# An expert layer with arms chosen at run time: the next expert's first steps queued in front of the jumps, and waits at the first exponential moved

## The reference

```python
x = x + relu(batchnorm(aggregate(ln(x)) @ W_l.T + b_l + ln(x) @ W_r.T))   # graph stage
xf = ln(x); logits = xf @ gate_w.T + gate_b                                # route
topk_val, topk_idx = top_k(logits, 2); probs = softmax(topk_val)
for kk in range(2):
    for e in range(4):
        mask = idx == e
        eo = _expert(xf, mask, ...)        # 8 heads, keys masked by mask
        out = out + where(mask, eo * w, 0)
x = x + out

def _expert(xf, mask, ...):
    h = ln(xf) * ln1_w + ln1_b
    q, k, v = split(h @ ipw.T + ipb)
    a = softmax(where(mask, q @ k.T / sqrt(64), NEG))
    x1 = xf + (a @ v) @ opw.T + opb
    return x1 + gelu(ln2(x1) @ w1.T + b1) @ w2.T + b2
```

## Time and profile before

| | |
|---|---|
| median of 3 runs | 1213.86 us (1209.42 to 1222.64) |
| profiled execution | 1213.72 us |
| its span | 1212.0 us |
| PE busy | 986.6 us, 81% |
| DVE busy | 720.9 us, 59% |
| ACT busy | 511.5 us, 42% |
| POOL busy | 496.6 us, 41% |
| mean granted TensorE clock | 0.910 |

### The profile page before, as it was taken

The page is one execution under the profiler, slowest core; times in us unless marked ns, Lnnn a source line. Parts: engine busy times, 40 slices in busy tenths (PEclk is TensorE's granted clock), DMA queues, the critical chain, the costliest instruction groups (busy, mean ns, idle before and its releaser), DMA issues.

```text
span 1212.0 us, 25215 instructions
## 1 busy us (share of the span) xinstructions
PE 986.6 (81%) x7268; PEld 572.8 (47%) x7269; DVE 720.9 (59%) x1723; ACT 511.5 (42%) x980; POOL 496.6 (41%) x455
## 2 busy tenths in 40 slices
PE   3897899999926677877788788888888889988786
PEld 2555567788513234433444334444444445534443
DVE  4597536441483576746865665665747458646743
ACT  2301122221423356325644426685858742336631
POOL 2102434452647444204531116473838752306641
PEclk9998889998957886999878898999999899989997
DMA  5491000000357410511134110000000032200011
GB/s 162 121 272 43 2 1 0 0 0 1 136 157 197 133 54 19 210 64 35 35 124 165 59 37 19 1 2 1 0 0 0 18 136 105 92 28 2 1 35 36
DMA packets 34850, 75.88 MB, mean 63 GB/s; under 512 B 8203, under 2 KB 8501, under 8 KB 34474
## 3 DMA queue, kind: packets, MB, share of 16 engines
q1 hardware_dynamic: 26122, 55.91, 14.8%
q0 software_dynamic: 8320, 16.49, 4.4%
q10 hardware_dynamic: 288, 2.10, 0.5%
HBM read 49.06 MB, written 26.70 MB: 63 GB/s over the span
## 4 chain that ended last, share of the span: by engine, by line
PE 54%; issue 14%; DVE 11%; ACT 8%; POOL 7%; DMA 2%; DVEq 1%; SPq 1%; ACTq 1%; POOLq 0%
PE bank L1465 17%; PE bank L1306 8%; PE bank L1346 6%; POOL p_lo L778 4%; PE bank L1642 3%; DVE mx L2338 2%; PE bank L1340 2%; ACT p_all L1058 2%; PE bank L1268 2%; PE bank L1525 2%; PE bank L1566 2%; POOL lists L730 1%; DVE mx L2478 1%; PE bank L1656 1%; PE bank L1548 1%
## 5 line engine op out<-in xcount | busy, mean ns | idle before, releaser
L778 POOL TENSOR_TENSOR p_lo<-p_all,p_hi 128x512 f16<-128x512 f32 (+2 forms) x240 | 253.3, 1069 | 263.7 <-ACT p_all L1058 262.1
L1055 ACT ACTIVATE p_hi<-bank 128x512 f16<-128x512 f32 (+2 forms) x240 | 131.7, 549 | 77.0 <-PE bank L1550 29.1
L2033 DVE TENSOR_SCALAR oh_src<-iota,edge 125x1250 f16 x178 | 106.0, 595 | 89.0 <-PE bank L1306 85.6
L1058 ACT ACTIVATE p_all<-bank 128x512 f32<-128x512 f32 (+2 forms) x240 | 131.2, 547 | 3.9 <-POOL p_lo L778 2.9
L1306 PE MATMUL bank<-oh_src,oh_dst 125*125 x534 | 108.8, 356 | 3.1 <-DVE oh_dst L2035 1.5
L2338 DVE TENSOR_REDUCE mx<-bank 128x1 f32<-128x512 f32 x144 | 87.2, 655 | 27.4 <-PE bank L1525 27.0
L1642 PE MATMUL bank<-hT,w 128*128 128x512 f16 x288 | 77.7, 405 | 24.3 <-ACT t L1102 18.9
L1465 PE MATMUL bank<-hT,w 128*128 128x256 f16 (+1 forms) x552 | 93.7, 335 | 3.9 <-issue 1.9
L1306 PEld LDWEIGHTS bank<-oh_src,oh_dst 125*125 x534 | 69.8, 141 | 41.9 <-issue 20.7
L1566 PE MATMUL bank<-v_hi,p_lo 128*128 128x65 f16 (+1 forms) x832 | 67.9, 199 | 22.6 <-POOL p_lo L778 20.1
L1566 PEld LDWEIGHTS bank<-v_hi,p_hi 128*128 128x128 f16 x832 | 49.8, 101 | 68.1 <-ACT p_hi L1055 31.4
(11 more groups left out here) (335 smaller groups left out, 1964.4 us busy)
## 6 DMA issues: line engine op xcount, KB each, us to landing
w_stage<-in_ew_dram SPq DMA_DIRECT2D x40, 512.0 KB, 4.4
lists<-zeros SPq DMA_DIRECT2D x1, 10340.0 KB
x_in<-lists SPq DMA_DIRECT2D x15, 517.0 KB, 6.6
x_mem<-lists SPq DMA_DIRECT2D x3, 1024.0 KB, 5.4
x_mem<-lists SPq DMA_DIRECT2D x1, 2560.0 KB, 9.7
out_dram<-x_mem SPq DMA_DIRECT2D x10, 250.0 KB
table<-rows SPq DMA_DIRECT2D x5, 449.8 KB
big<-in_x_dram SPq DMA_DIRECT2D x10, 224.0 KB
```

The source lines that it names most:

```text
L778: nc.gpsimd.tensor_tensor(p_lo[:, b % NPB, 0:cn], p_all[:, b % NP32, 0:cn], p_hi[:, b % NPB, 0:cn], ALU.subtract).then_inc(s_lo, 1)
L1055: nc.scalar.activation(p_hi[:, b % NPB, 0:cn], stb[b % 2][:, 0:cn], ACT.Exp).then_inc(s_exp, 1)
L1058: nc.scalar.activation(p_all[:, b % NP32, 0:cn], stb[b % 2][:, 0:cn], ACT.Exp).then_inc(s_all, 1)
L2033: nc.vector.tensor_scalar(oh_src[:, bass.ds(slot, 1), i, 0:N].rearrange("p a n -> p (a n)"), iota[:, :], edge[:, 0, i, bass.ds(g, 1)], Non ...
```

## The change

Five edits. `chosen` gets a function `ahead` that is emitted in front of each choice of an arm. ScalarE queues there the rows and the affine of the first two pairs, TensorE their turns and `value(0)`, VectorE the copy of `ep` and the four splits; what they queue is taken out of the arms. In the long arm the rows of pairs 2 and 3 are now both made ahead of the affine of pair 2, and in every arm stands a dummy activation `unread_e` with Exp. `WARM_NEXT` is gone. `bias_raw` moves to the last four tiles of `o_rows`, and ScalarE waits for `s_given` where it waited for `s_bias`. In the short arms the wait for `s_scat` goes to where `oT` is first written (j == 1); GpSimd's is dropped there, and in the long arm GpSimd waits for `s_bias` ahead of its low weights. In the first short head `side_of(1, 0)` and `side_of(1, 1)` are cut in halves of six matmuls, the first of them ahead of the heads.

```diff
--- before.py
+++ after.py
@@ -58,7 +58,7 @@
 LOW = 32
-WARM_SHORT, WARM_LONG, WARM_ROUTE, WARM_TURN, WARM_NEXT = 7, 12, 31, 5, 14
+WARM_SHORT, WARM_LONG, WARM_ROUTE, WARM_TURN = 7, 12, 31, 5
 UP = 5
...
@@ -135,6 +135,8 @@
 
+    if ahead is not None:
+        ahead(engine.snap(counter, min_val=0, max_val=NE - 1))
     choose("first")
@@ -201,7 +205,7 @@
         spot = sb("spot", [TT, 1], F32)
-        raised, unread = spot[0:1, :], spot[32:64, :]
+        raised, unread, unread_e = spot[0:1, :], spot[32:64, :], spot[64:96, :]
         slots = sb("slots", [TT, NT, 2], I32)
@@ -347,13 +351,13 @@
         p_all = sb("p_all", [P, NP32, 512], F32, attention)
-        bias_raw = p_all[:, 0, :]
         groups = ExitStack()
...
         o_rows = sb("o_rows", [P, NTL, P], F32, attention)
+        bias_raw = o_rows[:, NTL - 4:NTL, :].rearrange("p t n -> p (t n)")
         halves = sb("halves", [P, 2, 2, LW], F16, attention)
@@ -791,7 +795,6 @@
                 if shape.short:
-                    pool.wait_ge(s_scat, 16 * 2 * NT)
                     for u in range(H):
@@ -799,6 +802,8 @@
                 else:
+                    pool.wait_ge(s_bias, e + 1)
+                    pool.sem_inc(s_idle, 1)
                     for p in range(QKV_P, NWP):
@@ -988,36 +993,41 @@
 
+            def first_rows(e, p):
+                act.wait_ge(s_nr[p], 16 * (e + 1))
+                for t in (2 * p, 2 * p + 1):
+                    nc.scalar.activation(normal[:, t % 4, :], x_in[:, t, 0:D], ACT.Identity,
+                                         scale=x_in[:, t, D + 1:D + 2]).then_inc(s_n1, 1)
+
+            def ahead_act(e):
+                nc.scalar.activation(unread[:, :], ident[32:64, 0:1], ACT.Identity, scale=1.0)
+                act.wait_ge(s_msplit, msplit.at(0))
+                act.wait_ge(s_ln1, e + 1)
+                for p in range(AHEAD // 2):
+                    act.wait_ge(s_ahead[p], 32)
+                    first_rows(e, p)
+                for p in range(AHEAD // 2):
+                    scaled_columns(p, ep_ln1[:, 0:KC], ep_ln1[:, KC:2 * KC])
+
             def expert_act(e, shape):
...
                 ns, nq = len(spans), len(shape.queries)
-
-                def first_rows(p):
-                    if p < AHEAD // 2:
-                        act.wait_ge(s_ahead[p], 32)
-                    if p == AHEAD // 2:
-                        act.sem_inc(s_idle, 1)
-                        with nc.scalar.If(e < 1):
-                            act.wait_ge(s_ahead[2], 16 * (nt - AHEAD))
-                    act.wait_ge(s_nr[p], 16 * (e + 1))
-                    for t in (2 * p, 2 * p + 1):
-                        nc.scalar.activation(normal[:, t % 4, :], x_in[:, t, 0:D], ACT.Identity,
-                                             scale=x_in[:, t, D + 1:D + 2]).then_inc(s_n1, 1)
 
...
 
-                nc.scalar.activation(unread[:, :], ident[32:64, 0:1], ACT.Identity, scale=1.0)
-                act.wait_ge(s_msplit, msplit.at(0))
-                act.wait_ge(s_ln1, e + 1)
-                first_rows(0)
-                first_rows(1)
-                for p in range(np):
+                if np > AHEAD // 2:
+                    with nc.scalar.If(e < 1):
+                        act.wait_ge(s_ahead[2], 16 * (nt - AHEAD))
+                    first_rows(e, 2)
+                    first_rows(e, 3)
+                nc.scalar.activation(unread_e[:, :], ident[64:96, 0:1], ACT.Exp, scale=1.0)
+                for p in range(2, np):
                     scaled_columns(p, ep_ln1[:, 0:KC], ep_ln1[:, KC:2 * KC])
                     if p + 2 < np:
-                        first_rows(p + 2)
+                        first_rows(e, p + 2)
                 turned.skip(nt)
@@ -1127,6 +1137,8 @@
                         row_of(u + 1)
+                        if j == 1:
+                            act.wait_ge(s_scat, 16 * 2 * NT)
                         if j > 0:
@@ -1157,8 +1169,7 @@
                     row_of(0)
-                    act.wait_ge(s_bias, e + 1)
-                    act.wait_ge(s_scat, 16 * 2 * NT)
+                    act.wait_ge(s_given, e + 1)
                     for u in range(H):
@@ -1474,23 +1485,29 @@
 
+            def turn_first(p):
+                pe.wait_ge(s_n1, normed1.at(2 * p + 2))
+                for q in range(2):
+                    if p > 0:
+                        pe.wait_ge(s_affine, affine.at(2 * p + q - 1))
+                    turn(p, q)
+
+            def value(t):
+                pe.wait_ge(s_hsplit, hsplit.at(2 * (t // 2) + 2))
+                if t >= 2:
+                    pe.wait_ge(s_vcopy, vcopied.at(t - 1))
+                product(stb[t % 2][:, :], lambda a, c: hT[a][:, c, t * P:(t + 1) * P],
+                        lambda b, c: w16[:, b, c * 3 * D + 2 * D:(c + 1) * 3 * D], KC).then_inc(s_v, 1)
+
+            def ahead_pe(e):
+                for p in range(AHEAD // 2):
+                    turn_first(p)
+                pe.wait_ge(s_elo, e * NWP + QKV_P)
+                value(0)
+
             def expert_pe(e, shape):
...
                 ns, nq = len(spans), len(shape.queries)
-
-                def turn_first(p):
-                    pe.wait_ge(s_n1, normed1.at(2 * p + 2))
-                    for q in range(2):
-                        if p > 0:
-                            pe.wait_ge(s_affine, affine.at(2 * p + q - 1))
-                        turn(p, q)
-
-                def value(t):
-                    pe.wait_ge(s_hsplit, hsplit.at(2 * (t // 2) + 2))
-                    if t >= 2:
-                        pe.wait_ge(s_vcopy, vcopied.at(t - 1))
-                    product(stb[t % 2][:, :], lambda a, c: hT[a][:, c, t * P:(t + 1) * P],
-                            lambda b, c: w16[:, b, c * 3 * D + 2 * D:(c + 1) * 3 * D], KC).then_inc(s_v, 1)
 
@@ -1706,11 +1723,11 @@
                     if u == 0:
-                        side_of(1, 0, range(0, 12))
+                        side_of(1, 0, range(6, 12))
                     if hd == 0:
...
                         score_of(u + 1, 1)
-                    if j1 < H // 2:
+                    if j1 < H // 2 and u > 0:
                         side_of(j1, side, range(0, 4))
@@ -1721,7 +1738,7 @@
                     if j1 < H // 2:
-                        side_of(j1, side, range(4, 8))
+                        side_of(j1, side, range(4 if u > 0 else 0, 8 if u > 0 else 6))
                     short_sums(u, 1)
@@ -1731,7 +1748,7 @@
                     if j1 < H // 2:
-                        side_of(j1, side, range(8, 12))
+                        side_of(j1, side, range(8 if u > 0 else 6, 12))
                     if hd == 0:
@@ -1745,10 +1762,6 @@
 
-                turn_first(0)
-                turn_first(1)
-                pe.wait_ge(s_elo, e * NWP + QKV_P)
-                value(0)
                 if shape.short:
@@ -1764,6 +1777,7 @@
                     row_of(0)
+                    side_of(1, 0, range(0, 6))
                     pe.wait_ge(s_vcopy, vcopied.at(nt))
@@ -1895,9 +1909,6 @@
                         narrow(step - 3)
-                for k in range(WARM_NEXT):
-                    nc.tensor.matmul(sbk[k % 2][:, :], ident_h[:, :], hT[0][:, k % KC, 0:nt * P][:, 0:512], start=True,
-                                     stop=True)
                 biased.skip(nt)
...
@@ -2283,13 +2294,18 @@
 
+            def ahead_dve(e):
+                step(nc.vector.tensor_copy(ep[:, :].unsqueeze(1), epar[:, bass.ds(e, 1), :]))
+                step(nc.vector.tensor_scalar(ep[:, BQ:BK], ep[:, BQ:BK], HD ** -0.5, None, ALU.mult))
+                dve.sem_inc(s_ep, 1)
+                for p in range(AHEAD // 2):
+                    for q in range(2):
+                        split_columns(p, q)
+                steps.settle()
+
             def expert_dve(e, shape):
...
                 ns, nq = len(spans), len(shape.queries)
-                step(nc.vector.tensor_copy(ep[:, :].unsqueeze(1), epar[:, bass.ds(e, 1), :]))
-                step(nc.vector.tensor_scalar(ep[:, BQ:BK], ep[:, BQ:BK], HD ** -0.5, None, ALU.mult))
-                dve.sem_inc(s_ep, 1)
-
                 def parameters(cols, j):
...
```

More of the change, by code:

```diff
@@ L120, in __init__, with chosen @@
         assert len(self.rows) == self.nx and self.nx % 2 == 0 and self.nt % 2 == 0
-def chosen(nc, engine, name, arms):
+def chosen(nc, engine, name, arms, ahead=None):
     counter = engine.alloc_register(f"{name}_expert")
@@ L1218, in expert_act @@
                     r.settle()
-            for e, shape in chosen(nc, nc.scalar, "act", arms):
+            for e, shape in chosen(nc, nc.scalar, "act", arms, ahead_act):
                 expert_act(e, shape)
@@ L1912, in _ @@
             counts += [neg, splits]
-            for e, shape in chosen(nc, nc.tensor, "pe", arms):
+            for e, shape in chosen(nc, nc.tensor, "pe", arms, ahead_pe):
                 expert_pe(e, shape)
@@ L2529, in expert_dve @@
                     dve.sem_inc(s_pair, H // 2)
```

(7 more changed lines are left out.)

## The result

The changed kernel takes 1206.65 us in the median of 20 runs (1197.54 to 1223.42), the kernel before 1213.65 in 20 runs (1206.07 to 1228.85). The ratio is 0.9937, 95% interval 0.9912 to 0.9961: 7.6 us faster (4.7 to 10.7), a third of the 22.5 that I forecast, and outside my range. A second comparison of the same two programs gave 0.9974 (0.9942 to 1.0007), 3.2 us, an interval that just reaches no gain. So the gain is small, some 3 to 8 us.

A forecast was written before the change was run, and what follows sets the result against it. TensorE was taken as half the chain of waits, with engines' jumps last at expert entries; 7.0 + 4.2 + 1.2 + 0.2 + 4.7 + 3.0 + 2.2 = 22.5 us off gave 1191 us, range 1184 to 1201.

The forecast's parts named there:

- Part 3: Third expert's prelude: GpSimd's low weights wait for the bias steps, sparing VectorE's copies; gain 4.7 us (3.0 to 5.1).
- First entry: First expert: ScalarE's first rows no longer wait behind lookup and table load; gain 1.6 us (0.2 to 2.2).
- First head: First expert: exponentials no longer wait for bias steps and scatters; gain 5.4 us, 7.0 with the entry.
- part 4: First short heads: `side_of` halves reordered, 12 instead of 8 matmuls left behind; cost 0.9 us, 1.7 at half clock.
- Entry 2: Second expert: `ep` copy and `value(0)` start earlier, the jumps hidden behind; gain 4.2 us (2.5 to 5.9).
- VectorE's gap behind the fourth split: Sign at the entries: VectorE's jump moves there and shows as 4 us of idle time.
- Rival (c): Entries and preludes: without warm matmuls TensorE stays at half clock up to the heads; slower, 1232 us, chance 0.04.
- heads 2 and 4: Second and fourth expert: splits no longer wait on bias steps, less reordered products; gains 1.2 and 2.2 us.
- rival (a): Entries: the jump is only moved and ends last again behind `value(0)`; entries give 0, 1199 us, chance 0.15.
- the third entry: Third expert: ScalarE's jump, rows and table load give back the 4.4 us won; gain 0.2 us (-1.5 to 1.5).
- Entry 4: Fourth expert: `value(0)` starts 4.3 us earlier, but TensorE's jump follows it; gain 3.0 us (0.9 to 4.3).

The follow-up runs named there:

- old_sides: The change, but with `side_of(1,0)` and `side_of(1,1)` placed in the head as in the kernel before; 1197.46 us, ratio 0.9845.
- heads_only: The kernel before with only the new waits, GpSimd's weights and the `side_of` halves, jumps as before; 1212.23 us, ratio 0.9968.
- act_first: The change, but ScalarE jumps first as before and does its first pairs in the arm; 1211.85 us, ratio 0.9977.
- act_jump: old_sides, but from the second expert on ScalarE jumps first and does its first pairs in the arm; 1200.59 us, ratio 0.9844.
- all_four: old_sides with GpSimd held until `split_of(1,0)`, later bias steps, `value(0)` behind TensorE's jump, ScalarE jumping first from the second expert; 1212.63 us, ratio 0.9868.

## Why the prediction was wrong

**Kept.** Part 3: 4.7 forecast, 5.1 measured in prelude 3, by the mechanism named. First entry: the mechanism held, the size didn't. I wrote 1.6, but my own numbers give 1.1 (370.83 less 369.7); measured is 4.0, and ScalarE's first rows start 14.7 and 13.8 us behind the first gather instead of 17.7 and 17.1. First head: 5.4 forecast with part 4 in, about 3 measured; without part 4 it is 5.1 (13.6 for 18.7; two other kernels without it have 14.0 and 11.5). Entry 2's first 4.0 us were as forecast. VectorE's gap behind the fourth split is there, but longer: 8.88 us, a branch of 5.91 and a second stop of 2.58 in the arm, where I expected 4; the chain of waits doesn't pass through it. Rival (c), half clock through whole preludes, did not occur.

**Failed, step 1: part 4 and the heads.** I had "leave 12 instead of 8 matmuls of `side_of(1,1)` behind that point: 0.9 at full clock, 1.7 at half" and concluded 1.2 and 2.2 of gain in heads 2 and 4. Measured is a loss of 1.5 and 1.8; without part 4 the gain is 2.4 and 1.9. Part 4 costs 3.9 in each (old_sides) and some 2 in head 1, where the spread is as large: about 10 us in all by stages, and 0.9% by the two ratios. This is the largest part of the shortfall: of 15 us, 9 are in the three heads. I priced matmuls moved, not the gap that they had filled: taken out from behind the second score they leave TensorE empty until VectorE's maxima are done. And I moved GpSimd's work by the same 3.3 us as the exponentials without asking what it lands on, although part 3 had just been priced by that very contention. I wrote "some contention" for the first expert and put none in the others' terms.

**Failed, step 2: what hides TensorE's jump.** "TensorE's branch of 0.21 hides under it": the branch took 3.4 to 5.7 in all twelve profiles of other kernels (0.21 and 0.22 in both executions of before), even in heads_only (4.18), whose jumps are as before. So rival (a) held at the second expert; it got no price in the sum, and I put it at 0.15. The Trainium skill (Runtime: NRT & Kernel Launch, Instruction fetch mechanics) states that a taken branch beyond the sequencer's small buffer waits for a DMA fetch. The traces agree that the branch stalls (4.10 in the rows above); that the stall is a fetch no run here shows. Entry 2 gave 2.8 or 0.2 instead of 4.2.

**Failed, step 3: the third entry.** Forecast 0.2, measured -4.0. The order in line was right, the durations were not: ScalarE's stall went from 2.66 to 5.37, VectorE's from 3.19 to 5.60, TensorE's from 4.70 to 6.04, and all three now start within 1.8 us of each other. Moving ScalarE's away brings its stall back to 2.66, 2.38 and 2.37 (act_first, act_jump, all_four). That stalls side by side lengthen each other would fit this, but other rows speak against it. At the second and fourth entry ScalarE, TensorE and VectorE jump as close together, and ScalarE's stall is 2.4 to 3.3 there in every kernel in which it works ahead (4.2 to 5.4 at the third). VectorE's is 5.94 in all_four, almost alone. TensorE's is 3.80 in act_first and 6.58 in act_jump, with the same order of jumps. So which term failed is known, ScalarE's jump, put at 3.2 and measured at 5.6 of idle time, with TensorE's put at 4.70 and measured at 6.04; why they grew is open.

**Entry 4**: 3.0 forecast. 1.2 by the mean, but the two profiles of before differ by 2.6 there, so no more can be said than that it is between -0.1 and 2.5.

In sum 4.0 + 3.0 (head 1, mean) + 1.5 - 1.5 - 4.0 + 5.1 + 1.2 - 1.8 = 7.5, against the timed 7.6; so close a fit is partly luck, with stages that spread by 2 us and more. What stays open: what sets the length of a stall, and what the 14 warm matmuls did. No run keeps them beside the work ahead, and `value(0)` of the third expert varies by itself: 2.76 and 4.42 in the two profiles of before, 4.36 in the change.

## What to carry to other kernels

Work put in front of a jump covers it only from the moment that the sequencer reaches the branch: 3.4 and 3.5 us here with one product and with two, 1.8 at full clock. So price a jump at its longest row, not at a lucky 0.21, and count how much of the work is still to run when the branch begins. Staggering the engines' jumps gave back the third entry here (21.4), but no time in total. Before filling work is moved to an earlier place, ask what the engine will do in the wait that it leaves, and at which clock it comes back. When a wait is removed on one engine, follow everything that it was holding back: here it released GpSimd onto VectorE's copies, and the contention that part 3 cured in the third expert came back in the heads of the other three.

## What was not expected of the hardware

- A VectorE copy of 64x512 in f16 takes 0.28 us alone, 1.00 to 1.15 beside a GpSimd subtraction, and 3.35 beside four of them in a row (398.91 in the second profile of the change). The longest ends 0.15 us after GpSimd's series does.
- Sequencer stalls behind the same branch (L134) in the 14 profiles: ScalarE 2.4 to 2.7 where it jumps first, and where it works ahead 2.4 to 3.3 at the second and fourth entry but 4.2 to 5.4 at the third. VectorE 2.8 to 3.4 in the three profiles without work ahead and 4.7 to 6.4 in the eleven with it, with one exception (2.86 at old_sides' second expert). GpSimd 2.5 to 3.6 at the third and fourth entry, and 0.25 in all 14 profiles at the second, where the arm is the one that it has just left.
- The same 12 matmuls of `side_of` took 2.77 behind a gap of 1.17 us and 4.45 behind one of 2.12, at granted clocks of 1.00 and 0.62. Over the nine profiles with `value(0)` in front of the jump, second and fourth entry, it was at full clock (2.75 or 2.76) behind all five gaps of 0.45 to 1.17, and at half clock (4.3 to 4.9) behind twelve of the thirteen gaps of 2.0 to 5.5; the exception is act_first's second entry (2.23).
